# Nine float32 matmuls per group of a Flamingo layer, as three float32r passes each

## The reference, cut to what matters

```python
xf = _rms(x, n2_w).reshape(-1, C)             # the normalised state, 128 features
logits = jnp.nan_to_num(xf @ gate_w.T)        # the router: 4 experts
...                                           # softmax, the best two, their weights wts
o0 = _gelu(xf @ e0_up.T) @ e0_down.T
o1 = _silu(xf @ e1_w1.T) * (xf @ e1_w2.T) @ e1_down.T
o2 = _gelu(_gelu(_gelu(xf @ e2_l1.T) @ e2_l2.T) @ e2_l3.T) @ e2_l4.T
o3 = _gelu(_gelu(xf @ e3_down.T) @ e3_up.T) @ e3_out.T
moe = wts[:, 0:1] * o0 + wts[:, 1:2] * o1 + wts[:, 2:3] * o2 + wts[:, 3:4] * o3
```

## Time and profile before

| | us |
|---|---|
| median of 3 runs | 1200.54 (1198.05 to 1200.64) |
| the profiled execution | 1201.37 |
| its span, first to last instruction | 1199.6 |
| PE busy in the span | 1030.4 (86%) |
| PE weight loads | 623.6 (52%) |
| DVE busy | 828.7 (69%) |
| ACT busy | 740.2 (62%) |
| POOL busy | 346.7 (29%) |

### The profile page before, as it was taken

How to read it: one execution, slowest core, us unless ns; L and a number is a source line. 1 busy time by engine, 2 the same in 40 slices (tenths; PEclk the granted TensorE clock), 3 DMA queues, 4 the chain that set the end, 5 groups by cost and what they waited for, 6 DMA issues and landing times. The chain is left out here.

```text
span 1199.6 us, 26646 instructions
## 1 busy us (share of the span) xinstructions
PE 1030.4 (86%) x8578; PEld 623.6 (52%) x8578; DVE 828.7 (69%) x2264; ACT 740.2 (62%) x1329; POOL 346.7 (29%) x513
## 2 busy tenths in 40 slices
PE   2365779999999899999989899999989899988797
PEld 1133445555556555555556555555556555555454
DVE  6237577777787877777787877777787777764523
ACT  1144466766676676766676776766676776755343
POOL 4610323314141513314141513214131514213030
PEclk9576789999999999999999999999999999999799
DMA  4325343343444434243444434243444433221300
GB/s 155 54 70 136 101 118 102 96 111 71 114 118 115 118 96 107 83 112 67 114 118 115 118 102 106 85 106 67 114 117 115 118 106 102 86 43 53 63 10 10
DMA packets 78549, 114.28 MB, mean 95 GB/s; under 512 B 9136, under 2 KB 41520, under 8 KB 78384
## 3 DMA queue, kind: packets, MB, share of 16 engines
q1 hardware_dynamic: 78368, 111.58, 36.7%
q10 hardware_dynamic: 144, 2.21, 0.5%
HBM read 58.97 MB, written 53.74 MB: 94 GB/s over the span
## 5 line engine op out<-in xcount | busy, mean ns | idle before, releaser
L701 ACT ACTIVATE probs<-ps_s2a 120x512 f32<-120x512 f32 (+1 forms) x256 | 152.9, 597 | 81.1 <-PE ps_s2a L1056 72.7
L822 DVE TENSOR_REDUCE mpadA<-ps_w 128x4 f32<-128x480 f32 x256 | 150.4, 651 | 54.7 <-PE ps_w L1038 54.7
L822 DVE TENSOR_REDUCE mpadB<-ps_w 128x4 f32<-128x512 f32 x256 | 158.8, 683 | 29.1 <-PE ps_w L1038 29.1
L701 ACT ACTIVATE probs<-ps_s2b 120x512 f32<-120x512 f32 (+1 forms) x256 | 152.5, 596 | 0.0
L1103 PE MATMUL ps_w<-W,hid 128*128 128x96 f32 x1024 | 129.9, 281 | 15.1 <-ACT hid L697 10.9
L608 POOL TENSOR_SCALAR_AFFINE_SELECT probs<-probs 128x1024 f32<-128x1024 f32 x128 | 140.1, 1094 | 0.0
L1103 PEld LDWEIGHTS ps_w<-W,hid 128*128 128x128 f32 x1024 | 120.6, 194 | 36.2 <-issue 26.2
L574 POOL TENSOR_TENSOR rB<-veB,neg_half 128x4 f32<-128x4 f32 x16 | 16.1, 1008 | 400.9 <-DVE veB L725 400.9
L1121 PE MATMUL ps_w<-xfT,W 128*128 128x512 f32 x160 | 85.1, 621 | 0.0
L697 ACT ACTIVATE hid<-ps_s2a 128x512 f32<-128x512 f32 x80 | 47.8, 598 | 51.6 <-PE ps_s2a L1114 39.7
L1056 PE MATMUL ps_s2a<-qdA,kstA 128*120 128x512 f32 x128 | 69.4, 542 | 11.4 <-DMA qdA<-mTA 5.0
(11 more groups left out here) (184 smaller groups left out, 2119.6 us busy)
## 6 DMA issues: line engine op xcount, KB each, us to landing
scratch_Aq<-split_q SPq DMA_DIRECT2D x48, 256.0 KB, 2.4
qdA<-scratch_Aq SPq DMA_DIRECT2D x64, 192.0 KB
scratch_Bq<-split_q SPq DMA_DIRECT2D x48, 256.0 KB, 2.4
scratch_Bk<-split_k SPq DMA_DIRECT2D x48, 256.0 KB, 3.0
qdB<-scratch_Bq SPq DMA_DIRECT2D x64, 192.0 KB
kstB<-scratch_Bk SPq DMA_DIRECT2D x64, 192.0 KB
scratch_Ak<-split_k SPq DMA_DIRECT2D x48, 240.0 KB, 2.9
kstA<-scratch_Ak SPq DMA_DIRECT2D x64, 180.0 KB
```

What stands on the lines that cost most here:

```text
L701: nc.scalar.activation(probs[0:k, slot_of(part, *index), :], bank[0:k, :], ACT.Exp, scale=SCALE if part == "A" else 1.0).then_inc(done, 1)
L822: nc.vector.tensor_reduce(mneg[OP[part]][:, :, c, b], bank[:, 0:HT * k].rearrange("p (h k) -> p h k", h=HT), AX.X, ALU.max, negate=True).t ...
```

## The change

The nine fills read two tiles in place of one: `xh`, the state rounded to float32r, and `xl`, the rest. The weights are split in the same way, once, in setup. Each fill is then three float32r matmuls into one PSUM bank: high x high, high x low, low x high. The router's four matmuls stay float32 and become eight, four on `xh` and four on `xl`, added up in PSUM. ACT writes `xh` from the bank; DVE, behind it, writes `xl` from the bank and `xh`, and it is now DVE that sets `drained`. `hb` becomes the buffer `xn`, and `sq` becomes the buffer `split["q"]`, for which POOL waits until the stores from it have landed. The weights' order in memory is changed so that the five that are split lie together.

```diff
+        first, width = sum(n for _, n in WCOLS[:8]), 4 * HID + P
+        raw = W[:, first:first + width]
+        high, low = sb("high", [P, width], F32R), sb("low", [P, width], F32R)
+        at, upper = 0, {}
+        for name, n in WCOLS[8:13]:
+            upper[name] = (high[:, at:at + n], low[:, at:at + n])
+            at += n
+        xh, xl = sb("xh", [P, TOK], F32R), sb("xl", [P, TOK], F32R)
...
+        hb = xn
...
-        sq = sb("sq", [P, G, 2 * P])
+        sq = split["q"][:].rearrange("p s (b d) -> p (s b) d", d=2 * P).bitcast(F32)
...
-                        pool.tensor_tensor(sq[:], qk[:], qk[:], ALU.mult).then_inc(sq_ready, 1)
+                        pool.wait_ge(split_stored["q"], uses_of_split(st, "B") * USE_STORED)
+                        pool.tensor_tensor(sq, qk[:], qk[:], ALU.mult).then_inc(sq_ready, 1)
...
                     elif (part, work) == ("N", "k"):
                         queries_or_keys(st, "N", "A", "k", bias=col["bk"])
+                        if st.first("N"):
+                            act.wait_ge(weights_loaded, 16)
+                            nc.scalar.activation(high[:], raw, ACT.Copy).then_inc(upper_high, 1)
...
-                        nc.scalar.activation(xfT[:], bank[:], ACT.Identity, scale=col["n2"]).then_inc(done, 1)
+                        nc.scalar.activation(xh[:], bank[:], ACT.Identity, scale=col["n2"]).then_inc(xh_ready, 1)
...
+                        if work == "k" and st.first("N"):
+                            dve.wait_ge(upper_high, 1)
+                            nc.vector.tensor_tensor(low[:], raw, high[:].bitcast(F32), ALU.subtract).then_inc(upper_split, 1)
...
+                    elif (part, work) == ("D", "xfT"):
+                        dve.wait_ge(xh_ready, g + 1)
+                        nc.vector.scalar_tensor_tensor(out=xl[:], in0=bank[:], scalar=col["n2"], in1=xh[:].bitcast(F32),
+                                                       op0=ALU.mult, op1=ALU.subtract).then_inc(done, 1)
...
                     elif (part, work) == ("D", "xfT"):
+                        if st.first("D"):
+                            pe.wait_ge(upper_split, 1)
...
-                            ins = mm(bank[:, b * P:b * P + E], xfT[:, b * P:(b + 1) * P], w["gate"][:, 0:E], start=True, stop=True)
+                            for part_of_x in (xh, xl):
+                                ins = mm(bank[:, b * P:b * P + E], part_of_x[:, b * P:(b + 1) * P].bitcast(F32), w["gate"][:, 0:E],
+                                         start=part_of_x is xh, stop=part_of_x is xl)
...
-                        mm(bank[:], w[name][:, c * P:(c + 1) * P], xfT[:], start=True, stop=True).then_inc(done, 1)
+                        wh, wl = (half[:, c * P:(c + 1) * P] for half in upper[name])
+                        mm(bank[:], wh, xh[:], start=True, stop=False)
+                        mm(bank[:], wh, xl[:], start=False, stop=False)
+                        mm(bank[:], wl, xh[:], start=False, stop=True).then_inc(done, 1)
```

More of the change, by code:

```diff
@@ L64 @@
 WCOLS = [("Wq", P), ("Wk", P), ("Wv", P), ("Wo", P), ("wqk", 2 * P), ("wv", P), ("wo", UP), ("gate", P),
-         ("e0_up", HID), ("e1_w1", HID), ("e1_w2", HID), ("e2_l1", HID), ("e2_l2", 2 * HID), ("e2_l3", 2 * HID),
-         ("e3_down", P), ("e3_up", HID),
+         ("e0_up", HID), ("e1_w1", HID), ("e1_w2", HID), ("e2_l1", HID), ("e3_down", P), ("e2_l2", 2 * HID), ("e2_l3", 2 * HID),
+         ("e3_up", HID),
          ("down0", 2 * UP), ("down1", 2 * UP), ("down2", 2 * UP), ("down3", 2 * UP)]
@@ L279, in build @@
             at += n
+        first, width = sum(n for _, n in WCOLS[:8]), 4 * HID + P
+        assert WCOLS[8][0] == "e0_up" and WCOLS[12][0] == "e3_down"
+        raw = W[:, first:first + width]
[5 more added lines that the diff above has]
+        xh, xl = sb("xh", [P, TOK], F32R), sb("xl", [P, TOK], F32R)
         vc = sb("vc", [P, len(VCOLS)])
@@ L295, in build @@
         of_head, pick = sb("of_head", [P, NT, HT]), sb("pick", [P, HT])
-        xt, xb, xn, x1, xc, x2, yb, ym, hb = (sb(n, [P, G, P]) for n in ("xt", "xb", "xn", "x1", "xc", "x2", "yb", "ym", "hb"))
+        xt, xb, xn, x1, xc, x2, yb, ym = (sb(n, [P, G, P]) for n in ("xt", "xb", "xn", "x1", "xc", "x2", "yb", "ym"))
+        hb = xn
         ctT = sb("ctT", [DC, CT])
-        xnT, xfT = (sb(n, [P, TOK]) for n in ("xnT", "xfT"))
+        xnT = sb("xnT", [P, TOK])
         hT = sb("hT", [P, TOK])
@@ L374, in build @@
         masked = sem("masked")
+        upper_high, upper_split, xh_ready = sem("upper_high"), sem("upper_split"), sem("xh_ready")
         causal_ready, causal_chain = sem("causal_ready"), sem("causal_chain")
@@ L794, in step @@
                             block_diagonal_keys(part, "B", g)
+                    elif (part, work) == ("D", "xfT"):
+                        dve.wait_ge(xh_ready, g + 1)
+                        nc.vector.scalar_tensor_tensor(out=xl[:], in0=bank[:], scalar=col["n2"], in1=xh[:].bitcast(F32),
+                                                       op0=ALU.mult, op1=ALU.subtract).then_inc(done, 1)
                     elif (part, work) == ("B", "sums"):
                         dve.wait_ge(sq_ready, g + 1)
-                        nc.vector.tensor_reduce(hs[:], sq[:].rearrange("p b (h d) -> p (b h) d", d=HD), AX.X, ALU.add)\
+                        nc.vector.tensor_reduce(hs[:], sq.rearrange("p b (h d) -> p (b h) d", d=HD), AX.X, ALU.add)\
                             .then_inc(hs_ready, 1)
```

## The result

The changed kernel takes 1222.67 us in the median of 4 runs (1218.29 to 1224.59) against 1199.74 before, with a fourth run added to the three: 1.0183 times as long, with a 95% interval of 1.0161 to 1.0205. It is slower, as forecast (1213.4), but by 22.9 us and not 12.9, and 1.67 us above the range.

What follows compares the result with a forecast made beforehand. Bound: PE's chain of work plus its waits for DVE and ACT. Fourteen steps at +0.72 us (+10.1), the fifteenth group +1.9, the last +0.9: +12.9 on 1201.37 gives 1214.3, less 0.83 for the median: 1213.4 us, range 1200 to 1221.

Steps and rivals of the forecast that it cites:

- The drain of bank `w2`: DVE's pass behind ACT's read-out makes `estimate` 2 start later on PE: +0.75 us a step (0.60 to 0.80).
- rival 1: The later drain ahead of `estimate` 2 is hidden by other work and the rest cancels: 1201.3 us; chance 0.09.
- The router's matmuls: Sixteen router instructions instead of eight, with as many weight loads, on PE's path: +0.91 us a step (0.87 to 0.95).
- Which fills count: Of nine fills a step, four ahead of `wo` 1 and `e0_up` 1 shorten the path: 0.95 us of 1.71.
- Rival 2: PE's work itself bounds the loop, so all nine fills count and the kernel gets faster: 1196.1 us; chance 0.09.
- What one saves: Three float32r passes take 0.645 to 0.69 us against 0.86 for a float32 fill: 0.17 to 0.215 saved, 0.19 taken.
- passes more than 0.25 us apart: Sign in the profile after, in the fills on PE, that would show the forecast wrong; forecast fills took 0.65 to 0.69 us.
- Rival 3: Fill passes don't hide their weight loads, 0.32 us each, so a step gets +2.16: 1235 us; chance 0.07.
- The step's bounds: With all bounds together a loop step adds 0.37 to 1.07 us, giving a range of 1207 to 1219 us.
- The last two groups: Groups behind the fourteen steps: the fifteenth, in the drained pipeline at half clock, +1.9 us; the last +0.9 us.
- Fourteen steps like the loop's: Fourteen of the sixteen groups pass part D in steps like the loop step profiled: +10.1 us together.
- The rest: Setup's split, the squares' wait for a store, `xh` and `xn`: no cost, at most +1.4 us for setup.

Runs made afterwards that it cites:

- experiment 2: Changed kernel with the bank set free by ACT, DVE's same-size pass reading another SBUF tile: 1212.38 us, 1.0100 of before.
- experiment 1: Changed kernel with the router's matmuls on the high half alone, eight instructions a group instead of sixteen: 1207.77 us, 1.0063 of before.
- experiment 3: Changed kernel with the bank set free by ACT and the router on the high half alone, three-pass fills kept: 1193.14 us, 0.9950 of before.
- experiment 4: Changed kernel with each fill as one float32 matmul call of the high halves, drain and router as changed: 1230.20 us, 1.0243 of before.
- Experiment 6: Kernel before the change with each of the router's matmuls done twice, sixteen instructions a group: 1221.29 us, 1.0201 of before.

## Why the prediction was wrong

The mechanism and the sign were right: the wait for the bank, the sixteen router instructions and the fills that count lie where they were put. Two terms were mis-sized, and fourteen steps were taken for alike that are not.

- *The drain of bank `w2`*: +0.75 forecast. `estimate` 2 waits 0.76 us for DVE's `xl`; 0.68 stay on the path, and experiment 2 takes 0.68 back. Right; rival 1 is out.
- *The router's matmuls*: +0.91 forecast; 0.90 in the timeline, 0.89 in experiment 1. Right.
- *Which fills count*: right. `e1_w2` 1 ends in a wait for DVE's `on`, and the wait ahead of `hT` grew from 0.41 to 0.56 us. Rival 2 is out.
- *What one saves*: **this step failed**: "a fill saves 0.17 to 0.215. I take 0.19." The four fills on the path, each with the distance from the work ahead of it, save 0.17, 0.11, 0.11 and 0.16 us: 0.55 and not 0.76, and from `oT` 1 to `nT` 1 it takes 0.06 longer. With the last fill's 0.17 the fills are worth 0.64 us a step (experiment 3; 0.60 in experiment 4) and not 0.95. I counted each of the three passes at 0.215 to 0.23. The passes start at 594.25, 594.56 and 594.79, and the next work at 595.03: 0.31 + 0.23 + 0.24 = 0.78 us, against 0.86 for the float32 fill. The first takes 0.31, as the first `s2` did, where I had put 0.10 us down to its own load and then left that out; so the sign of being wrong, "passes more than 0.25 us apart", came true in it. Where the first pass comes right behind another fill's last one, as in `e3_down`, it takes 0.25 (602.64 to 602.89). That the load is the reason is not tested. Rival 3 (no load hidden) is out: 0.23 a pass behind the first. The rule that stood beside it, of the Trainium skill's page "TensorE: Matmul & The Clock Gate", section "The mechanism", is not borne out here: these passes all use full rows, and the load of the second starts at 594.33, 0.08 us behind the start of the first.
- *The step's bounds*: the terms with their own bounds (0.60 to 0.80, 0.87 to 0.95, five fills at 0.17 to 0.215) add up to 0.40 to 0.90 us, not to the 0.37 to 1.07 of the sum. The measured 0.95 lies above them.
- *The last two groups*: **this term failed too**, and it is the larger part in the first profile. +1.9 and +0.9 forecast. In the second profile they come to +2.9 and +0.9; in the first to +6.3 and +2.3. PE is at half clock for 31 us of group 14 there, against 17 in the second profile and 14 before. I had priced the half clock where it lay before, and not a second fall of it, from 1153 to 1166.
- *Fourteen steps like the loop's*: the first lost 2.6 us and the 13th 1.8, instead of 0.7. Some 0.8 us of each is DVE's copy behind POOL's mask pass, shown above. The rest of the first goes with the clock, which stood at 0.50 to 0.53 in its first 10 us against 0.84 and 0.78 before. Such a start is not the change's own doing alone: experiment 3, without the two costs, has it too (0.50 and 0.54).
- *The rest* (setup, the squares' wait, the shared buffers): nothing that shows, as forecast. The two passes in setup took 1.16 and 1.35 us, POOL never waits for a store, and filling the pipeline took no longer.

The profiled execution lies 23.2 us above that of before, 10.3 more than the sum's 12.9. Of these, 2.5 are the fills, in eleven loop steps; 5.8 are the last two groups; 1.6 are the copy in two steps; the half clock of the first step makes up about what filling the pipeline gave back. The part with the clock differs from execution to execution: the second profile of the changed kernel took 1217.52 us, 7 less with an equal loop, and lies inside the range. Experiment 6, which has sixteen router instructions and nothing else of the change, shows the same kind of loss in the same places. What in the change makes half clock last longer there is not settled: shortening the router did not end it in group 14, setting the bank free early shortened group 14 in one profile (62.2) and not in another (65.7).

## What to carry to other kernels

A pass split off for accuracy has to be produced, and the producer's place matters more than the matmuls: here nine cheaper fills saved 0.64 us a step, while one more reader of a PSUM bank on the path and eight more weight loads for a four-column product cost 1.57. Look first for who waits for the bank: a DVE pass of the same length that does not hold the bank cost nothing (experiment 3). Made by POOL in SBUF, with the router on the whole state, the same split cost nothing either, and the kernel became 0.3% faster than before. And when passes are priced, count the first with its load: take the distance from the start of the work ahead to the start of the work behind, not that between two passes. Last, a loop step is no price for the steps at the pipeline's ends: here two of them lost 0.8 us more because a short copy had slipped behind another engine's pass.

## What the runs showed of the hardware

Accumulating float32r passes of 512 columns start 0.23 to 0.24 us apart at full clock behind the first, which takes 0.31; the two instructions of a float32 matmul make 0.43 each. So three passes take 0.78 us where the float32 fill took 0.86.

The clock can fall in the middle of a loop, with PE busy throughout the 2 us ahead of it (2.00 of 2.00). Behind sixteen matmuls of four columns, which ran at 1.00 and kept the weight loads busy too (1.99 of 2.00 us), it stood at half (0.53 over 3.6 us) in three of eleven loop steps of one profile and in two of another, never the same ones. In the other steps of these two profiles it did not fall behind the same work. With a wait of 0.76 us for DVE a little ahead of the sixteen, as in the changed kernel, it never fell in the loop in two profiles; nor with eight instructions, nor with the sixteen in two lots (one profile), nor in two profiles of the kernel before with the router twice, where float32 fills follow. What sets it off is open.

A DVE copy of 128x128 float32 in SBUF, 0.23 us by itself, that starts while a POOL mask pass of 1.09 us runs ends 0.08 us behind that pass: 1.03 us here. This is read from rows and not tested by a run.
